# Rows gathered as 128-byte float32 features into four buffers, and turned two slots at a time

## The chip, the cores and the metric

The kernel runs on one core of one Trainium2 chip. The metric is the time of one execution on the device, in microseconds (us). Engines are named PE (TensorE, matrix products), DVE (VectorE), ACT (ScalarE), POOL (GpSimd) and SP (SyncE); ns are nanoseconds.

## The reference

A graph of 3125 nodes with 32 features each and 100000 edges, sorted by their destination `dst`, goes through four layers. Each layer adds its result to `x` and normalizes.

```python
def edge_mlp(x, src, dst):                     # layer 0
    msg = concat([x[dst], x[src] - x[dst]])    # 64 numbers an edge
    h = relu(msg @ W1 + b1); h = relu(h @ W2 + b2); h = relu(h @ W3 + b3)
    return segment_mean(h @ W4 + b4, dst)

def gcn(x, src, dst):                          # layers 1 and 2: weighted sums over edges
    return segment_sum(scaled(x)[src], dst)    # layer 2: then @ weight + bias, relu

def gatv2(x, src, dst):                        # three times in layer 3
    xl, xr = x @ Wl, x @ Wr                    # 8 heads of 32
    logits = (leaky_relu(xl[src] + xr[dst]) * att).sum(-1)
    alpha = softmax over the edges of one dst
    return segment_sum(alpha * xl[src], dst).mean(heads) + bias
```

The three attention layers have a self loop for each node, a residual and a batch norm.

## The kernel before

Nodes lie in 25 windows of 128 (`W`). The edges are cut into blocks of 256 that belong to one window of destinations each; a block has two slots of 128 edges, one edge to a partition. Eight slots are a group, and there are `G` = 104 groups (832 slots). All loops below run over groups.

An edge needs the features of its source. There are two ways to them. **Gather:** POOL issues one indirect DMA for each slot (`DMA_INDIRECT`), which fetches for each of the 128 partitions the row of `table` that its entry of `idx` names. **Dense reading:** PE multiplies a one-hot matrix of the edges' sources (made by DVE from `r_dram`) with the whole table in SBUF, 12 bf16 matmuls, and DVE picks and sums one of seven candidates. `table` in DRAM has rows of `TAB` = 80 float32: 32 features, and behind them the same features as three bf16 parts (hi, mid, lo) whose sum is the float32 number. 

The features of the destination come from windows: SP loads the three parts of a group's four windows (`load_windows`, tile `xwin`), and PE multiplies them with a one-hot matrix of the destinations (`turned`), 12 matmuls for each group.

**Edge pass** (`pool_edges`, `sp_pass0`, `act_pass0`, `pe_pass0`; 104 steps). Seven of a group's slots are gathered (L368) into one of three buffers `rows`, the eighth is read densely (L811, L1478, L1483) into `one0`. `rows_in` of PE turns the group into bank 0 of PSUM: sources of side 0 on partitions 0 to 31 and of side 1 on 64 to 95, destinations on 32 to 63 and 96 to 127. A row slot is turned by three bf16 matmuls with 128x32 weights against `identb`, one for each part (L831); the dense one by a float32 product (L835). The order of these and of the window matmuls (L827) is the list `TURNS`, which alternates rows and windows and the two sides, so that they use different columns of the array. ACT copies the bank to `xT`; three layers of products follow (L842, L847, L855), and a product with the one-hot matrix of the destinations sums the group (L864), which DVE adds to `acc`.

**Convolutions** (twice). 72 groups are gathered whole by POOL (L398) into four buffers, 32 groups are read densely (L900).

**Attention** (three layers, `pool_attention`, `sp_attention`, `act_attention`, `pe_attention`, `attention` of DVE). POOL gathers a group (L381) into one of two buffers: 8 slots of even groups, 7 of odd ones, whose eighth is read densely (`stationary_one`, `read_one` L1029, `pick_one` L1756 and L1759). A buffer is free when PE has turned it (`x_made`, `rows_in` with `TURNS`, L974, L980, L986) and ACT has copied its features to `xs` (`keep`, L651, semaphore `xs_kept`). Step u of PE is, in order: half of the projection (`z_half`, L994), the self loops in the first steps, in even steps the dense reading of group u+3, the first half of the weighted sums of group u-10 (L1055), in odd steps `linear` (L1005), the second `z_half`, `rows_in` of group u+1, the second half of the sums, in odd steps the logits (L1015). Each 8 groups are a chunk; at its end DVE scans the logits for the maxima and PE turns them back and forth (L1099, L1107, L1117). The last 10 steps have sums alone. Between layers the sums become features (`pe_attention_out`), the batch norm runs, and `give_table` of DVE makes the parts for the next layer's table; `store_table` of SP stores it, and POOL waits for that store.

Each engine runs its own program in a fixed order; semaphores tie them. POOL's whole program after the start is gathers and waits. SP's queue has, for attention step u, the four windows and two halves of `turned` of group u+2 and the two halves of `hot` (one-hot matrices) of group u-8.

Of the kernel before, what the change touches and what calls it, by code (L numbers as in the profile page):

```python
# [25 lines left out]
P = 128  # L26
# [34 lines left out]
TAB = C + 3 * C // 2  # L61
# [6 lines left out]
TURNS = [x for i in range(2) for x in [("row", 2 * i, 0), ("window", i, 0), ("row", 2 * i, 1), ("row", 2 * i, 2), ("window", i, 1),  # L68
                                       ("row", 2 * i + 1, 0), ("row", 2 * i + 1, 1), ("window", i, 2), ("row", 2 * i + 1, 2)]]
# [4 lines left out]
def build(nc, x, edge_blocks, L0, W_gcn, b_gcn, gat, out):  # L74
    with ExitStack() as ctx:
# [3 lines left out]
        def sem(name):  # L79
# [29 lines left out]
        rows = sb("rows", [P, 3, 8, TAB])  # L109
        x0_dram = nc.dram_tensor("x0_dram", [P, W * C], F32).ap()  # L110
# [9 lines left out]
        identb = sb("identb", [P, P], BF16)  # L120
# [37 lines left out]
        spanhot = sb("spanhot", [P, HALF, GROUPS], BF16)  # L158
# [57 lines left out]
        one0 = o1[:, 2064:2064 + 4 * C].rearrange("p (b c) -> p b c", b=4)  # L216
# [4 lines left out]
              for k in range(2)]  # L221
        rows4 = [rows[:, 0, :, :], rows[:, 1, :, :]] + [o0[:, 5120 + 640 * k:5120 + 640 * (k + 1)].rearrange(
            "p (j c) -> p j c", j=8) for k in range(2)]
# [10 lines left out]
        tabC = o0[:, 1024:1024 + W * 48].bitcast(BF16).rearrange("p (w c) -> p w c", w=W)  # L234
        cand = o0[:, 2224:2224 + GROUPS * C].rearrange("p (g c) -> p g c", g=GROUPS)
        bt1 = [o0[:, 2560 + 1024 * k:2560 + 1024 * (k + 1)].bitcast(BF16).rearrange("p (k n e) -> p k n e", k=FOLD, n=4)
               for k in range(2)]
        rline1 = [T2[:, :, :].rearrange("p w c -> p (w c)")[:, 64 + 256 * k:320 + 256 * k].bitcast(F16) for k in range(2)]
        hotb = o1[:, 2560:3584].bitcast(BF16).rearrange("p (b j n) -> p b j n", b=2, j=8)
        rowparts = [rows[:, b, :, :].rearrange("p j c -> p (j c)").bitcast(BF16).rearrange("p (j c) -> p j c", j=8)  # L240
                    for b in range(3)]
# [41 lines left out]
        gathered = [sem(f"gathered{b}") for b in range(3)]  # L283
        rows_in3 = [sem(f"rows_in3_{b}") for b in range(3)]
        x0_stored, x0_in = sem("x0_stored"), sem("x0_in")
# [33 lines left out]
        r1_in = [sem(f"r1_in{b}") for b in range(2)]  # L319
        bt1_made, one_read, one_picked, one_kept = sem("bt1_made"), sem("one_read"), sem("one_picked"), sem("one_kept")  # L320
        tab_kept = sem("tab_kept")
# [16 lines left out]
        scaled, norm_turned, x_given, tab_copied = sem("scaled"), sem("norm_turned"), sem("x_given"), sem("tab_copied")  # L338
# [16 lines left out]

        def rows_there(l, g):

            n = l * G + g
            return rows_in3[n % 2], 16 * sum(8 - k % 2 for k in range(n % 2, n + 1, 2))

        def pool_edges(pool):

            pool.wait_ge(table_stored, 16)
            for g in range(G):
                if g >= 3:
                    pool.wait_ge(x0_made, 4 * (g - 2))
                for j in range(7):
                    pool.indirect_dma_start(  # L368
                        rows[:, g % 3, j, :], None, table,
                        bass.IndirectOffsetOnAxis(ap=idx[:, 8 * g + j:8 * g + j + 1], axis=0)).then_inc(gathered[g % 3], 16)  # L370

        def pool_attention(pool, l):

            pool.wait_ge(table_stored, 16 * (l + 4))
            for g in range(G):
                n = l * G + g
                if n >= 2:
                    pool.wait_ge(x_made, 4 * (n - 1))
                    pool.wait_ge(xs_kept, n - 1)
                for j, s in enumerate(piece_slots(g)[0:8 - g % 2]):  # L380
                    pool.indirect_dma_start(  # L381
                        rows[:, n % 2, j, :], None, table,
                        bass.IndirectOffsetOnAxis(ap=idx[:, s:s + 1], axis=0)).then_inc(rows_in3[n % 2], 16)
# [46 lines left out]
        def load_windows(sp, codes, at, b):  # L430

            code = sp.value_load(codes[0:1, at], min_val=0, max_val=(1 << 20) - 1)
            for k in range(4):
                w = window_of(sp, code, k)
                sp.dma_start(xwin[:, b, k, :], table[bass.ds(w * P, P), C:TAB].bitcast(BF16)
                             ).then_inc(xwin_in[b], 16)

        def sp_pass0(sp):
# [23 lines left out]
            def windows_for(g):  # L462
                if g >= G:
                    return
                if g >= 2:
                    sp.wait_ge(x0_made, 4 * (g - 1))
# [25 lines left out]
        def sp_attention(sp, l):  # L492
            sp.wait_ge(table_stored, 16 * (l + 4))

            def rows_for(g):
                b, c, n = g % 2, g // 8, piece_of(g)
                if l * G + g >= 2:
                    sp.wait_ge(x_made, 4 * (l * G + g - 1))
# [15 lines left out]
            def numbers_for(c):  # L514
                if c >= CHUNKS:
                    return
                at = l * CHUNKS + c
                if at >= 2:
                    sp.wait_ge(bt1_made, FOLD * (at - 1))
                first = CHUNK * c + CHUNK // 2 + 4 * PIECE + PIECE - 1  # L520
                sp.dma_start(rline1[at % 2].rearrange("p (n e) -> p n e", n=4),
                             r_dram.rearrange("a (f e) -> (a f) e", f=2)[first:first + 13:4, :].partition_broadcast(P)
# [1522 lines left out]
```

## Time and profile before

| | |
|---|---|
| timed runs, median of 3 | 5986.88 us (5984.18 to 5997.32) |
| profiled execution, span (no other time of it is shown) | 7770.9 us |
| PE busy | 5760.6 us, 43965 matmuls |
| DVE busy | 3565.2 us |
| ACT busy | 1748.7 us |
| POOL busy | 4059.1 us, 4236 instructions |
| edge pass, convolutions, attention begin (first gather) | 52.6, 1331.8, 3218.2 us |

The profiled execution is longer than a timed run, by 30%. Times of single instructions are from it. A time line has start and length in us, the engine, the line of the kernel, output<-input, the count of instructions merged, and in brackets the idle time before them and what ended it; "issue" there means that nothing the profile shows was waited for, "remote" or "another core or an unknown queue" that the releaser isn't among what was recorded. A float32 matmul counts as two instructions, a float32 transpose as one. Ends of matmuls are modelled and overlap the next start; distances between starts are the safer measure.

### The profile page before, as it was taken

To read this page: it belongs to the slowest core of one execution; us is meant where nothing else is said; L and a number is where in the kernel's file an instruction comes from. 1 tells how busy PE (TensorE), PEld (TensorE's weight loads), DVE (VectorE), ACT (ScalarE), POOL (GpSimd) and SP (SyncE) were. 2 spreads that over 40 slices of the span, in tenths; PEclk is the share of its full clock that TensorE was granted. 3 is DMA by queue.
4 is the path that set the end of the run, shared out by engine and by line. 5 is a ranking of instruction groups with operands and counts; after the bars stand their busy time and mean duration, and the time that the engine had idled before them with its cause. 6 is when DMAs were issued, how large, how long until landed. Compare 5 with 4: busy or idle time off the path is not lost.

```text
span 7770.9 us, 130521 instructions
## 1 busy us (share of the span) xinstructions
PE 5760.6 (74%) x43965; PEld 3691.2 (48%) x43965; DVE 3565.2 (46%) x6811; ACT 1748.7 (23%) x3748; POOL 4059.1 (52%) x4236
## 2 busy tenths in 40 slices
PE   5888886566646666578887876877787758788777
PEld 4666665455545454334444443444444424444444
DVE  5444444455544444444444444444444534444446
ACT  2222222344420000022222221222222122222221
POOL 4555554666646566455555533555555245555551
PEclk8888887777767776688888897888888878888988
DMA  4444443222212222233333332333333223333332
GB/s 103 129 129 129 128 128 98 51 56 56 56 47 56 55 56 55 49 82 93 88 91 88 89 85 56 90 90 89 92 89 89 80 58 92 89 89 93 91 88 65
DMA packets 688913, 648.23 MB, mean 83 GB/s; under 512 B 401396, under 2 KB 483771, under 8 KB 688251
## 3 DMA queue, kind: packets, MB, share of 16 engines
q1 hardware_dynamic: 548266, 463.96, 20.0%
q0 software_dynamic: 135616, 175.22, 11.8%
q8 instruction: 357, 5.85, 0.3%
q14 instruction: 306, 2.50, 0.1%
q10 hardware_dynamic: 4368, 0.70, 0.1%
HBM read 550.21 MB, written 89.17 MB: 82 GB/s over the span
## 4 chain that ended last, share of the span: by engine, by line
PE 43%; issue 22%; another core or an unknown queue 21%; DVE 9%; ACT 3%; DVEq 2%; DMA 0%; POOL 0%; ACTq 0%; POOLq 0%
PE ps L1055 14%; PE ps L900 7%; PE ps L994 5%; PE ps L1005 2%; PE ps L1015 2%; PE ps L855 2%; PE ps L915 1%; PE ps L980 1%; DVE region L1778 1%; DVE acc L1803 1%; PE ps L974 1%; PE ps L864 1%; ACT region L662 1%; PE ps L811 1%
## 5 line engine op out<-in xcount | busy, mean ns | idle before, releaser
L381 POOL DMA_INDIRECT rows<-table,idx x2340 | 2258.3, 965 | 2221.5 <-ACT region L651 1042.6
L1055 PE MATMUL ps<-region,hot 128*128 128x272 f32 x4992 | 1528.3, 457 | 295.8 <-DVE region L1756 159.4
L1055 PEld LDWEIGHTS ps<-region,hot 128*128 128x128 f32 x4992 | 1040.8, 219 | 690.9 <-issue 461.8
L1803 DVE TENSOR_TENSOR acc<-acc,ps 128x272 f32 x1248 | 544.5, 436 | 1685.6 <-remote 808.6
L662 ACT ACTIVATE region<-ps 128x512 f32<-128x512 f32 x1248 | 677.3, 595 | 2691.7 <-remote 1438.8
L900 PE MATMUL ps<-hot,region 128*128 128x192 bf16 (+1 forms) x6144 | 896.1, 309 | 444.2 <-issue 429.0
L900 PEld LDWEIGHTS ps<-hot,region 128*128 128x128 bf16 x6144 | 703.4, 123 | 590.9 <-issue 529.9
L368 POOL DMA_INDIRECT rows<-table,idx x728 | 696.6, 957 | 534.2 <-PE ps L835 320.4
L994 PE MATMUL ps<-xT,wcat 64*128 64x512 f32 x2496 | 771.8, 696 | 170.4 <-issue 92.1
L1778 DVE TENSOR_TENSOR region<-ps,region 128x1056 f32<-128x1056 f32 x582 | 724.7, 1251 | 44.0 <-issue 40.4
L398 POOL DMA_INDIRECT rows<-table,idx x576 | 546.6, 949 | 378.5 <-issue 157.3
L398 POOL DMA_INDIRECT region<-table,idx x576 | 548.3, 952 | 342.5 <-issue 158.1
L980 PE MATMUL ps<-identb,rows 128*32 128x128 bf16 x7020 | 405.7, 236 | 290.9 <-issue 251.5
L980 PEld LDWEIGHTS ps<-identb,rows 128*32 128x32 bf16 x7020 | 263.1, 102 | 625.7 <-issue 624.8
L974 PE MATMUL ps<-turned,xwin 128*32 128x256 bf16 x3744 | 394.8, 304 | 133.7 <-issue 131.1
L994 PEld LDWEIGHTS ps<-xT,wcat 64*128 64x128 f32 x2496 | 211.5, 204 | 550.0 <-issue 525.8
L1635 DVE TENSOR_TENSOR region<-ps,gmask 128x448 f32<-128x448 f32 x256 | 158.7, 620 | 620.9 <-remote 551.9
L709 ACT ACTIVATE region<-iota,region 128x128 bf16<-128x128 f32 x832 | 254.1, 389 | 536.4 <-remote 394.5
L1015 PE MATMUL ps<-region,attblk 128*32 128x512 f32 x2496 | 323.7, 627 | 8.0 <-ACT region L662 5.1
L855 PE MATMUL ps<-w,region 128*128 128x64 f32 x1664 | 293.1, 349 | 21.6 <-ACT region L641 15.9
L855 PEld LDWEIGHTS ps<-w,region 128*128 128x128 f32 x1664 | 276.1, 259 | 50.8 <-ACT region L641 43.4
L1615 DVE TENSOR_TENSOR acc<-acc,ps 128x96 f32 (+1 forms) x832 | 192.1, 231 | 228.0 <-issue 77.3
(304 smaller groups left out, 6646.9 us busy)
## 6 DMA issues: line engine op xcount, KB each, us to landing
hot<-hot_dram SPq DMA_DIRECT2D x624, 256.0 KB
turned<-turned_dram SPq DMA_DIRECT2D x624, 128.0 KB
rows<-table,idx POOLq DMA_INDIRECT x3644
hot_dram<-hot SPq DMA_DIRECT2D x104, 512.0 KB
xwin<-table SPq DMA_DIRECT2D x1664, 24.0 KB
region<-hot_dram SPq DMA_DIRECT2D x64, 512.0 KB
region<-d_dram SPq DMA_DIRECT2D x104, 256.0 KB
turned_dram<-turned SPq DMA_DIRECT2D x104, 256.0 KB
```

Source lines behind the costliest of these rows:

```text
L368: pool.indirect_dma_start(rows[:, g % 3, j, :], None, table, bass.IndirectOffsetOnAxis(ap=idx[:, 8 * g + j:8 * g + j + 1], axis=0)).then_i ...
L381: pool.indirect_dma_start(rows[:, n % 2, j, :], None, table, bass.IndirectOffsetOnAxis(ap=idx[:, s:s + 1], axis=0)).then_inc(rows_in3[n % ...
L398: pool.indirect_dma_start(rows4[at % 4][:, j, :], None, table, bass.IndirectOffsetOnAxis(ap=idx[:, 8 * g + j:8 * g + j + 1], axis=0)).then ...
L662: act.activation(rz[g % 2][:, 2 * t + side, :], ps[:, Z + side, :], ACT.Relu).then_inc(rz_made, 1)
L855: mm = pe.matmul(ps[:, 7, j * HID:(j + 1) * HID], h2[:, at:at + P], w3[:, :], start=True, stop=True)
L900: mm = pe.matmul(ps[:, GB + i % 2, 224 * j:224 * j + n], bt[b][:, k, at:at + P], tabparts[:, k::FOLD, (2 + s) * C:(3 + s) * C], start=(k = ...
L980: mm = pe.matmul(ps[q:q + C, XT, j * P:(j + 1) * P], rowparts[(l * G + g) % 2][:, at, 2 * C + s * C:2 * C + (s + 1) * C], identb[:, :], st ...
L994: pe.matmul(ps[:, Z + side, :], wcat[l][q:q + 64, side, t * P:(t + 1) * P], xT[q:q + 64, g % 2, :], start=True, stop=True).then_inc(z_summ ...
L1015: pe.matmul(ps[at:at + 32, LG, :], attblk[l][:, t, (3 - m) * H:(7 - m) * H], rz[g % 2][:, 2 * t + side, :], start=False, stop=(m == 3 and ...
L1055: mm = pe.matmul(ps[:, sum_bank(k, side, i), 0:PC + H], hot[:, b, 4 * side + 2 * i + j, :], px[b][:, 4 * side + 2 * i + j, :], start=(j == ...
L1778: v.tensor_tensor(to, at.unsqueeze(3).broadcast_to([P, 4, H, HK]), xs[:, (k // 8) % 2, k % 8, 4 * side:4 * side + 4, :].unsqueeze(2).broad ...
L1803: v.tensor_tensor(at, at, ps[:, sum_bank(k, side, i), 0:PC + H], ALU.add).then_inc(att_added, 1)
```

## The change

- The edge pass gathers rows of 32 float32 (128 bytes) straight from the input `x`; each attention layer from an array of its own, `feats[l]`, to which SP stores `X`. `table` holds the three bf16 parts alone (`TAB` = 48 float32, 192 bytes), for the windows and the convolutions.
- `rows` has four buffers (`RING`), in the edge pass and in the attention; each slot has 64 columns, of which the upper 32 stay zero after one clearing at the start. `place` puts the slots of side 0 on even and of side 1 on odd places, so that two neighbours together are 128 columns.
- PE turns two slots at once with a float32 transpose of 128x128 (`turn_rows`, four for each group, with zeros where the destinations go), and the window matmuls write their quarters behind it (`turn_windows`).
- The dense reading in the attention is gone, with its one-hot matrices, its DMAs and its picks; POOL gathers 8 slots of each group there. The edge pass keeps its dense reading of the eighth slot, whose sum goes into the row buffer.
- ACT's copy of the features into the table is gone. The copy of X for the end comes from `feats[0]`.

```diff
-TAB = C + 3 * C // 2
+TAB = 3 * C // 2
+RING = 4
+TURN = 3
+WINDOWS = [(side, i, s) for i in range(2) for s in range(3) for side in range(2)]
...
+        feats = [nc.dram_tensor(f"feats{l}", [W * P, C], F32).ap() for l in range(LAYERS)]
...
-        rows = sb("rows", [P, 3, 8, TAB])
+        rows = sb("rows", [P, RING, 8, 2 * C])
...
+        def place(j):
+            return 2 * (j % 4) + j // 4
...
         def pool_edges(pool):
-            pool.wait_ge(table_stored, 16)
+            pool.wait_ge(rows_cleared, 1)
             for g in range(G):
-                if g >= 3:
-                    pool.wait_ge(x0_made, 4 * (g - 2))
+                if g >= RING:
+                    pool.wait_ge(x0_made, TURN * (g - RING + 1))
                 for j in range(7):
                     pool.indirect_dma_start(
-                        rows[:, g % 3, j, :], None, table,
+                        rows[:, g % RING, place(j), 0:C], None, x,
...
         def pool_attention(pool, l):
-            pool.wait_ge(table_stored, 16 * (l + 4))
+            pool.wait_ge(feats_stored, 16 * (l + 1))
             for g in range(G):
                 n = l * G + g
-                if n >= 2:
-                    pool.wait_ge(x_made, 4 * (n - 1))
-                    pool.wait_ge(xs_kept, n - 1)
-                for j, s in enumerate(piece_slots(g)[0:8 - g % 2]):
+                if n >= RING:
+                    pool.wait_ge(x_made, TURN * (n - RING + 1))
+                    pool.wait_ge(xs_kept, n - RING + 1)
+                for j, s in enumerate(piece_slots(g)):
                     pool.indirect_dma_start(
-                        rows[:, n % 2, j, :], None, table,
+                        rows[:, n % RING, place(j), 0:C], None, feats[l],
...
             for l in range(LAYERS):
+                sp.wait_ge(x_given, 3 + l)
+                sp.dma_start(feats[l].rearrange("(w p) c -> p w c", p=P), X[:, :, :]).then_inc(feats_stored, 16)
                 store_table(sp, 3 + l)
...
+        def turn_rows(pe, bank, b, made):
+            for j in range(4):
+                mm = pe.transpose(ps[:, bank, j * P:(j + 1) * P], rows[:, b, 2 * j:2 * j + 2, :].rearrange("p a c -> p (a c)"),
+                                  ident[:, :])
+            mm.then_inc(made, 1)
+
+        def turn_windows(pe, bank, b, made):
+            for side, i, s in WINDOWS:
+                q = 64 * side
+                mm = pe.matmul(ps[q + C:q + 2 * C, bank, 2 * i * P:2 * (i + 1) * P], xwin[:, b, 2 * side + i, s * C:(s + 1) * C],
+                               turned[:, b, (4 * side + 2 * i) * P:(4 * side + 2 * i + 2) * P], start=(s == 0), stop=(s == 2))
+                if i == 1 and s == 2:
+                    mm.then_inc(made, 1)
...
-                for kind, j, s in TURNS:
...
+                turn_rows(pe, XT, g % RING, x_made)
+                turn_windows(pe, XT, b, x_made)
...
-            def read_one(g):
...
-            def stationary_one(l, c, k):
...
-            def pick_one(l, g):
...
-            v.tensor_copy(tabC, tabparts[:, :, 2 * C:5 * C]).then_inc(tab_kept, 1)
```

## Rows read from the trace of the kernel before

**Rows 1.** The page: its first line, and part 4 by engine

```profile
span 7770.9 us, 130521 instructions
PE 43%; issue 22%; another core or an unknown queue 21%; DVE 9%; ACT 3%; DVEq 2%; DMA 0%; POOL 0%; ACTq 0%; POOLq 0%
```

**Rows 2.** Groups by line: count | busy us, mean ns | idle before

```profile
L381 POOL DMA_INDIRECT rows<-table,idx x2340 | 2258.3, 965 | 2221.5 <-ACT region L651 1042.6 <-issue 784.5 <-DMA table<-hot 319.7
L368 POOL DMA_INDIRECT rows<-table,idx x728 | 696.6, 957 | 534.2 <-PE ps L835 320.4 <-issue 192.4 <-DMA table<-hot 19.5
L398 POOL DMA_INDIRECT region<-table,idx x576 | 548.3, 952 | 342.5 <-issue 158.1 <-PE ps L927 129.2 <-remote 55.2
L398 POOL DMA_INDIRECT rows<-table,idx x576 | 546.6, 949 | 378.5 <-issue 157.3 <-PE ps L927 128.4 <-remote 55.4
L980 PE MATMUL ps<-identb,rows 128*32 128x128 bf16 x7020 | 405.7, 236 | 290.9 <-issue 251.5 <-DMA rows<-table,idx 38.5
```

**Rows 3.** Waits of POOL: us in total, times, longest

```profile
POOL rows L381 <- ACT region L651: 1042.6, 254, 10.6
POOL rows L381 <- DMA table<-hot: 319.7, 3, 131.8
POOL rows L368 <- issue: 192.4, 626, 0.6
```

**Rows 4.** Gathers of two lines: duration ns min/median/max

```profile
L381 POOL DMA_INDIRECT rows<-table,idx x2340: 938/944/1928, 3218.2 to 7639.8; - x195
...
L415 POOL DMA_INDIRECT region<-in_edge_blocks,block_no x4: 937/942/1134, 28.2 to 32.2; - x4
```

**Rows 5.** Time line of POOL: start us, us, instruction, [idle before <- releaser]

```profile
52.63 0.94 POOL L368 DMA_INDIRECT rows<-table,idx  x1 [19.53 <-DMA table<-hot]
...
106.63 0.94 POOL L368 DMA_INDIRECT rows<-table,idx  x1 [27.47 <-PE ps L835]
...
1262.91 0.94 POOL L368 DMA_INDIRECT rows<-table,idx  x1 [0.30 <-issue]
...
1331.75 0.95 POOL L398 DMA_INDIRECT rows<-table,idx  x1 [28.73 <-DMA table<-hot]
...
2217.36 0.94 POOL L398 DMA_INDIRECT region<-table,idx  x1 [0.30 <-issue]
...
2268.94 0.95 POOL L398 DMA_INDIRECT rows<-table,idx  x1 [8.67 <-DMA table<-hot]
...
3218.17 0.94 POOL L381 DMA_INDIRECT rows<-table,idx  x1 [57.22 <-DMA table<-hot]
...
4738.70 0.94 POOL L381 DMA_INDIRECT rows<-table,idx  x1 [130.66 <-DMA table<-hot]
...
7639.78 0.95 POOL L381 DMA_INDIRECT rows<-table,idx  x1 [0.30 <-issue]
```

**Rows 6.** Time line of PE, and of DVE for the last row

```profile
3856.34 1.21 PE L1029 MATMUL ps<-region 128*128 128x224 bf16 x12
...
4120.30 0.60 PE L1107 MATMUL ps<-ident,region 128*128 128x128 f32 x4
...
4120.83 0.64 PE L1015 MATMUL ps<-region,attblk 128*32 128x512 f32 x4
...
4613.92 1.13 PE L994 MATMUL ps<-xT,wcat 64*128 64x512 f32 x4
...
4618.07 0.23 PE L980 MATMUL ps<-identb,rows 128*32 128x128 bf16 x2
...
4618.90 2.10 PE L1055 MATMUL ps<-region,hot 128*128 128x272 f32 x8
...
4620.93 1.13 PE L994 MATMUL ps<-xT,wcat 64*128 64x512 f32 x4
...
4629.95 0.50 PE L1055 MATMUL ps<-region,hot 128*128 128x272 f32 x1
...
4728.57 0.98 DVE L1267 CAST hot<-X 128x800 bf16<-128x800 f32 x1
```

More of the change, by code:

```diff
@@ L221, in build @@
               for k in range(2)]
-        rows4 = [rows[:, 0, :, :], rows[:, 1, :, :]] + [o0[:, 5120 + 640 * k:5120 + 640 * (k + 1)].rearrange(
-            "p (j c) -> p j c", j=8) for k in range(2)]
+        rows4 = [o0[:, 5120 + 8 * TAB * k:5120 + 8 * TAB * (k + 1)].rearrange("p (j c) -> p j c", j=8) for k in range(4)]
         parts4 = [r.rearrange("p j c -> p (j c)").bitcast(BF16).rearrange("p (j c) -> p j c", j=8) for r in rows4]
@@ L282, in build @@
         idx_made = sem("idx_made")
-        gathered = [sem(f"gathered{b}") for b in range(3)]
-        rows_in3 = [sem(f"rows_in3_{b}") for b in range(3)]
-        x0_stored, x0_in = sem("x0_stored"), sem("x0_in")
+        rows_at = [sem(f"rows_at{b}") for b in range(RING)]
+        rows_cleared = sem("rows_cleared")
+        feats_stored, x0_in = sem("feats_stored"), sem("x0_in")
         hot_made = sem("hot_made")
@@ L434, in load_windows @@
                 w = window_of(sp, code, k)
[L435 removed]
+                sp.dma_start(xwin[:, b, k, :], table[bass.ds(w * P, P), :].bitcast(BF16)
                              ).then_inc(xwin_in[b], 16)
@@ L820, in rows_in @@
                 pe.wait_ge(xwin_in[b], 64 * (g // 2 + 1))
[L821 removed]
+                pe.wait_ge(*edge_rows(g))
                 pe.wait_ge(one0_kept, g + 1)
[L823 to L838 removed]
+                turn_rows(pe, 0, g % RING, x0_made)
+                turn_windows(pe, 0, b, x0_made)
             def first_layer(g):
@@ L1051, in sums_half @@
                         pe.wait_ge(att_added, of_bank)
-                    if side == 1 and i == 0:
-                        pe.wait_ge(one_picked, (l * G + min(k + LAG + 4, G)) // 2)
                     for j in range(2):
@@ L1296, in give_table @@
             def give_table(of, first=False):
-                hi, mid, lo = (tabparts[:, :, (2 + k) * C:(3 + k) * C] for k in range(3))
-                if first:
-                    cp(tab[:, :, 0:C], of)
-                else:
+                hi, mid, lo = (tabparts[:, :, k * C:(k + 1) * C] for k in range(3))
+                if not first:
                     v.sem_inc(x_given, 1)
@@ L1319, in _ @@
             v.memset(X[:, W - 1, :], 0.0).then_inc(x_zeroed, 1)
+            v.memset(rows[:, :, :, :], 0.0).then_inc(rows_cleared, 1)
             v.memset(zeros[:, :], 0.0).then_inc(zeros_made, 1)
@@ L1480, in pick0 @@
                 v.wait_ge(one0_picked, g + 1)
-                if g >= 4:
-                    v.wait_ge(x0_made, 4 * (g - 3))
-                v.tensor_reduce(one0[:, g % 4, :], cand0.rearrange("p g c -> p c g"), AX.X, ALU.add).then_inc(one0_kept, 1)
+                if g >= RING:
+                    v.wait_ge(x0_made, TURN * (g - RING + 1))
+                v.tensor_reduce(rows[:, g % RING, place(7), 0:C], cand0.rearrange("p g c -> p c g"), AX.X, ALU.add).then_inc(one0_kept, 1)
             def bias0(g):
@@ L1863, in attention @@
                         link(v.tensor_tensor(at, at, fscale[:, :].unsqueeze(2).broadcast_to([P, H, HK]), ALU.mult))
-                    def pick():
-                        if u % 2 == 0 and u + 3 < G:
-                            pick_one(l, u + 3)
-                    if phase in (3, 4) and u // 8 + 1 < CHUNKS:
-                        for q in range(2):
-                            stationary_one(l, u // 8 + 1, 2 * (phase - 3) + q)
                     if phase == 0 and ends:
@@ L1916, in _ @@
                 give_table(X[:, :, :])
[L1917 to L1925 removed]
+                for i in range(QUADS):
                     n = min(4, W - 4 * i)
```

175 lines of the change are left out of this document (19 added, 156 removed).

## The prediction

> **What bounds the kernel now.** I read the page's parts 1 and 4 first, then the groups, the waits of POOL, and time lines of POOL and PE.
>
> Its execution took 7770.9 us over its span, and the page shows nothing around that; the timed runs have a median of 5986.88 us, 0.770 of it. So 1784 us exist only under the profiler. The chain names PE first, but gives 21% (about 1630 us) to "another core or an unknown queue", and this program has one core [rows 1]. I read that share as PE held up while it is recorded, and take no duration from a stretch in which PE stutters. What I need is an engine whose times don't depend on PE's stutter. That is POOL.
>
> POOL issues 4220 gathers: 728 in the edge pass, 1152 in the two convolutions, 2340 in the attention [rows 2]. One takes 0.957, 0.949 to 0.952 and 0.965 us on average [rows 2], and the next begins 0.307 us later when nothing is to be waited for (192.4/626) [rows 3]. Gathers only: 728 x 1.264 + 1152 x 1.257 + 2340 x 1.272 = 920 + 1448 + 2976 = 5344 us. POOL is without gathers up to 52.6 us, then 67.9 (1263.9 to 1331.8), 50.6 (2218.3 to 2268.9), 319.7 in sum before the first gathers of the three layers [rows 3], and 130.2 us at the end, together 621; and 27.5 us in which three filled buffers wait for PE's first step [rows 5]. 5344 + 621 + 28 = 5993 us, against 5987 timed. All other waits of POOL in this trace (1043 us of them for the ACT copy that frees a buffer [rows 3]) have no room in a timed run. That it fits to 6 us is partly luck; that it fits to 1% says that POOL sets the time of the kernel without a profiler, if its spacing is the same there.
>
> PE is close behind. The cleanest stretch is the end of a layer, where its records come without a gap: an even step takes 4613.92 to 4620.93 = 7.01 us, an odd one to 4629.95 = 9.02 us, the latter without the row turns (0.83 us, 4618.07 to 4618.90) and without the dense reading (12 matmuls, 1.21 us to the end of the last; I take 1.1) [rows 6]. In sum 18.0 us for two steps, 9.0 a step; four groups of four turns for each chunk of 8 steps, at 0.53 us [rows 6], add 0.3 a step. POOL needs 7.5 x 1.272 = 9.5 us a step. The two are within 3%, POOL ahead.
>
> **The change, part by part.**
>
> *Dense reading out of the attention.* Each odd group gathers 8 rows instead of 7: 52 more in each layer, 156 in all, 156 x 1.272 = +198 us on POOL. In exchange PE loses 1872 matmuls (1.1 us x 156 = 172 us, 0.55 a step) and DVE three instructions for each reading. PE and DVE stand beside POOL, so this is worth nothing while POOL bounds.
>
> *128-byte rows in place of 320-byte ones.* One would hope for cheaper gathers. The trace has one of another size: the four gathers of edge blocks fetch 4096 bytes for each partition and take 0.942 us in the median, where those of table rows take 0.944 [rows 4]. The issue doesn't depend on the bytes. I take 0, bounds -0.01 and +0.01 us a gather. The traffic saved (192 bytes a row) lies on DMA engines that are no one's bound.
>
> *Whole-array turns.* PE loses 21 to 24 bf16 turns of a step (7020 in the attention [rows 2], 104 x 21 in the edge pass) and a float32 one; four float32 transposes of two slots each come in. Four such transposes take 0.53 us from the first to the next group (4120.30 to 4120.83) [rows 6]. The twelve window matmuls stay, but no longer beside row turns: at the reading's pace of about 0.09 us for 208 columns, 256 columns take 0.11 us, in six pairs 0.65 us. So 1.2 us where 0.83 stood, +0.35 us a step: fewer instructions, no less array time. Bounds: -1.2 us, if PE outside the profiler is held by the count of instructions, not by columns, and +0.8 us, should the windows run singly. I take +0.35. A step of attention then needs 9.3 - 0.55 + 0.35 = 9.1 us of PE against 8 x 1.272 = 10.2 of POOL.
>
> Of this the Trainium skill, TensorEngine Tiling, section Key Properties, says that changing the tiling mode, and not only the tile, drains the engine. The new order has one change of mode more in a step of attention (64x128, 128x128, 128x32). The trace agrees as far as it goes: after the last of four transposes the next mode begins 0.2 us later, where they follow each other at 0.11. That drain is inside the 0.53 us; by the page alone the direction would be the same, a costlier row turn.
>
> *Four buffers in place of three (edge) and two (attention).* Where POOL bounds it never waits for a buffer, and more of them don't speed it. They do help once: before the first edge step POOL stood 27.5 us with its buffers full [rows 5]; now it issues 7 more gathers in that time, 7 x 1.264 = -9 us. Between layers nothing can be fetched ahead, as the rows don't exist.
>
> *A table of rows of its own for each layer.* POOL waits for its store, issued when X is complete, instead of for the parts table. The first cast begins at 4728.57, the table's store waits for it and three more operations (four of 1 us each), and the gathers began at 4738.70 [rows 6, 5]; the new store can go some 4.2 us earlier, so -4.2 x 3 = -13 us. SP has one store more ahead of the table's, 0.4 us to issue; PE's first step needs both and still has 10 us of gathers to wait for. The gathers of the edge pass no longer wait for a table either, about 3 us earlier, but then into the same wait for PE.
>
> *The smaller edits.* ACT's copy of X into the table (0.9 us, beside DVE's casts), DVE's copy of the parts, a cast, the clearing of the row buffers at the start (beside the load of the edges): 0, bounds -5 and +5. The convolution's table is 0.6 MB instead of 1 MB: -3 us for two stores, bounds -8 and 0.
>
> Sum: 5987 + 198 - 9 - 13 - 3 = 6160 us. One term pulls it down. Gathers in the attention average 0.965 us over a median of 0.944; if all of this excess goes with the DVE work removed, 2496 x 0.021 = -52. I take a third: **6140 us**, +2.6%. In the profiled execution the sum runs otherwise. There PE is what is held up, and about 9900 of its matmuls go (7020 + 104 x 21 turns, 1872 in the readings, 520 for the eighth slots; 1664 transposes come); a step of 13.3 us (7639.8 - 3218.2, less the two pauses between layers, 319.7 - 57.2, over 312 [rows 5, 3]) falls to POOL's 10.2 and a little, so that its span should be 6500 to 7100 us, much shorter than 7771. Profile shorter, kernel slower.
>
> The Trainium skill, GPSIMD Engine Reference, section Key points, says that POOL shares its SBUF interfaces with VectorE and contends with instructions of the 2-port mode or with two SBUF inputs. No row here ties a long gather to a DVE instruction; by the page the excess should shrink, the sum would be 6108.
>
> **Rivals.**
>
> *A. PE bounds, and POOL's spacing is partly the profiler's.* If the 0.305 us between gathers is mostly recording, POOL needs 7.7 us a step after, and PE decides. For it: the chain, and 1043 us in which POOL waited for buffers that PE and ACT hold. Against it: PE's clean steps make 9.3 x 312 = 2900 us; with 649 around the gathers 2438 us are left for the edge pass and the convolutions, and their gathers alone need 2368 at the trace's spacing, but only 1790 without the 0.307. So three stages would have to miss POOL's time from above by chance. Time: by columns 312 x (0.35 - 0.55) + 104 x 0.35 - 13 - 9 = -48, 5940 us; if the count of instructions decides, up to -1.2 us a step of 416, 5987 - 500 - 172 = 5315, which the 4376 gathers, at 0.95 us and 600 us around them (4760), allow. The likelier end is the first; a middle spacing near 1.15 us also ends there.
>
> *B. POOL bounds, but at 1.20 us or so without the profiler.* Then 9.6 us a step after, against 9.5 before (PE and POOL together): +30 to +60 less 25, 5990 to 6020: hardly to be told from no change.
>
> *C. The turn costs more than it seems.* The side of slower, but by PE: the windows run after the transposes with a drain on each side, +0.8 us on 416 steps = +333, less 172 and 22: 6125 us. It decides once a PE step passes POOL's 10.2, so 1.1 us above my 9.1. The trace's drains of 0.2 us speak against that.
>
> *D. The change doesn't do what it says:* four buffers are of no use if the order of the queue still ties POOL to the step before. This is so under the forecast anyway, and costs the 9 us.
>
> **How the numbers follow.** Forecast 0.54; A 0.32; B 0.10; C 0.04. Of this kernel, about 0.2% (12 us) can be told from no change. Slower: 0.54 + 0.04 + half of B = 0.63; same 0.05; faster 0.32. The forecast's own range is 6085 to 6175: the terms' bounds, and a spacing at the median of 1.249 instead of the mean (4376 x 0.018 = -79) at its foot. To hold 8 in 10 the range reaches into the first half of A: 5890 to 6180.
>
> **What would show it.** Right: in the profile after, gathers still 0.94 us with 0.30 between, in the attention back to back with no wait for an ACT copy; 10.1 us a step; PE with gaps that end on gathers; the first gather of a layer about 6 us after X. The four transposes about 0.5 us and the windows 0.65. Wrong: a gather issue that is visibly shorter for 128 bytes; POOL waiting for buffers in spite of four; or a timed run below 5975, which can't be with 4376 gathers at 1.25 us and 600 us outside them (6070): then the spacing under the profiler isn't the kernel's.

## The result and the profile after

The changed kernel takes **6056.62 us** (median of 4 runs, 6054.66 to 6073.31) against 5992.10 for the kernel before on the same chip (4 runs): a ratio of 1.0117, interval 1.0100 to 1.0134. It is slower, as forecast, but by 64.5 us and not by 153: inside the range that was to hold 8 in 10 (5890 to 6180), below the forecast's own (6085 to 6175).

The page of the kernel after: its first line, part 4 by engine, and three groups.

```profile
span 6055.0 us, 109647 instructions
POOL 48%; issue 25%; PE 17%; DVE 7%; DVEq 2%; ACT 1%; ACTq 1%; DMA 0%; POOLq 0%
L375 POOL DMA_INDIRECT rows<-feats,idx x2496 | 2394.4, 959 | 1023.4 <-issue 759.4
L771 PE MATMUL ps<-ident,rows 128*128 128x128 f32 x1664 | 270.7, 287 | 320.4 <-DMA rows<-feats,idx 295.2
L779 PE MATMUL ps<-turned,xwin 128*32 128x256 bf16 x4992 | 363.0, 283 | 0.0
```

Its waits of POOL, and one of PE (us in total, times, longest):

```profile
POOL rows L375 <- issue: 759.4, 2491, 0.3
POOL rows L375 <- DMA feats<-X: 263.4, 3, 117.2
POOL rows L375 <- ACT region L627: 0.6, 2, 0.3
PE ps L771 <- DMA rows<-feats,idx: 295.2, 230, 16.6
```

Its time line of POOL (start us, us, instruction, the idle time before it and its releaser):

```profile
99.97 0.94 POOL L362 DMA_INDIRECT rows<-in_x,idx  x1 [13.36 <-PE ps L779]
...
3710.03 0.94 POOL L375 DMA_INDIRECT rows<-feats,idx  x1 [117.19 <-DMA feats<-X]
...
4877.64 0.94 POOL L375 DMA_INDIRECT rows<-feats,idx  x1 [117.05 <-DMA feats<-X]
...
5929.39 0.94 POOL L375 DMA_INDIRECT rows<-feats,idx  x1 [0.30 <-issue]
```

The time line of PE in a step of its attention:

```profile
3025.75 1.13 PE L945 MATMUL ps<-xT,wcat 64*128 64x512 f32 x4
3027.58 0.63 PE L771 MATMUL ps<-ident,rows 128*128 128x128 f32 x4 [0.70 <-DMA rows<-feats,idx]
3028.14 0.83 PE L779 MATMUL ps<-turned,xwin 128*32 128x256 bf16 x12
3028.90 2.10 PE L989 MATMUL ps<-region,hot 128*128 128x272 f32 x8
```

How they are read beside the rows of before. The profiled execution of after isn't stretched: its span and the timed runs agree. The stutter behind the 7770.9 us of [rows 1] isn't in it, and with it went "another core or an unknown queue". The attention's gathers still take 0.94 us (mean 0.959, 0.965 before [rows 2]) and follow each other after 0.30 us: 2491 of 2496 waited for nothing else, where 254 waited for a buffer in the stretched execution of before [rows 3]. So GpSimd does set the attention's pace after, and TensorE waits 295 us for rows. The turn with its windows takes 3028.90 - 3027.58 = 1.32 us, where 0.83 stood [rows 6].

A comparison by stages needs an undistorted profile of before. The first experiment, `before_ring4`, gives one: it is timed like before, and its span is 5983.2. From its profile and that of after, by the first gather of each stage (us):

```
stage                             before, 4 buffers  after     difference
start to first convolution        1051.4             1039.8    -11.6
both convolutions                 1510.7             1502.0     -8.7
layer 1 (with the pause behind)   1136.5             1168.2    +31.7
layer 2                           1143.1             1167.6    +24.5
layer 3 to the end                1141.5             1177.4    +35.9
sum                               5983.2             6055.0    +71.8
```

All the loss lies in the attention, 92 us in 312 steps. The first difference is the least certain one: in the six undistorted profiles of variants of before, whose edge pass is the same, the first convolution begins at 1045.9 to 1066.3 us.

### The profile page after: what moved, and what is told of

Its sections match the earlier page's. It is cut to its first block, busy times and chain, and to the rows that moved or that the text cites. A ratio compares the mean times of both kernels' runs of the same rounds, so it can differ in the third digit from the quotient of the medians.

```text
span 6055.0 us, 109647 instructions
## 1 busy us (share of the span) xinstructions
PE 4879.0 (81%) x34033; PEld 3210.5 (53%) x34033; DVE 3385.8 (56%) x6326; ACT 1790.5 (30%) x3743; POOL 4198.1 (69%) x4392
## 4 chain that ended last, share of the span: by engine, by line
POOL 48%; issue 25%; PE 17%; DVE 7%; DVEq 2%; ACT 1%; ACTq 1%; DMA 0%; POOLq 0%
POOL rows L375 39%; PE ps L869 10%; POOL rows L362 9%; DVE region L1575 2%; PE ps L896 1%; DVE region L1553 1%; PE ps L884 1%; DVEq L1527 1%; DVE acc L1533 1%; PE ps L833 1%; PE ps L824 1%; ACTq L714 1%; DVEq L1533 1%; PE ps L989 0%; PE ps L794 0%
## 5 line engine op out<-in xcount | busy, mean ns | idle before, releaser
L375 POOL DMA_INDIRECT rows<-feats,idx x2496 | 2394.4, 959 | 1023.4 <-issue 759.4
L989 PE MATMUL ps<-region,hot 128*128 128x272 f32 x4992 | 1304.9, 405 | 86.5 <-DVE acc L1696 75.1
L392 POOL DMA_INDIRECT region<-table,idx x1152 | 1092.4, 948 | 384.2 <-issue 350.5
L989 PEld LDWEIGHTS ps<-region,hot 128*128 128x128 f32 x4992 | 903.3, 190 | 499.4 <-issue 302.4
L362 POOL DMA_INDIRECT rows<-in_x,idx x728 | 701.3, 963 | 251.4 <-issue 220.4
L869 PE MATMUL ps<-hot,region 128*128 128x192 bf16 (+1 forms) x6144 | 742.5, 292 | 24.1 <-issue 22.9
L771 PE MATMUL ps<-ident,rows 128*128 128x128 f32 x1664 | 270.7, 287 | 320.4 <-DMA rows<-feats,idx 295.2
L896 PE MATMUL ps<-region 128*128 128x96 bf16 x1152 | 94.8, 242 | 524.4 <-issue 360.3
L771 PEld LDWEIGHTS ps<-ident,rows 128*128 128x128 f32 x1664 | 184.4, 147 | 570.9 <-issue 570.7
L779 PEld LDWEIGHTS ps<-turned,xwin 128*32 128x32 bf16 x4992 | 220.2, 99 | 93.5 <-issue 73.3
```

The lines of the kernel that those rows point to most:

```text
L362: pool.indirect_dma_start(rows[:, g % RING, place(j), 0:C], None, x, bass.IndirectOffsetOnAxis(ap=idx[:, 8 * g + j:8 * g + j + 1], axis=0) ...
L375: pool.indirect_dma_start(rows[:, n % RING, place(j), 0:C], None, feats[l], bass.IndirectOffsetOnAxis(ap=idx[:, s:s + 1], axis=0)).then_in ...
L392: pool.indirect_dma_start(rows4[at % 4][:, j, :], None, table, bass.IndirectOffsetOnAxis(ap=idx[:, 8 * g + j:8 * g + j + 1], axis=0)).then ...
L771: mm = pe.transpose(ps[:, bank, j * P:(j + 1) * P], rows[:, b, 2 * j:2 * j + 2, :].rearrange("p a c -> p (a c)"), ident[:, :])
L779: mm = pe.matmul(ps[q + C:q + 2 * C, bank, 2 * i * P:2 * (i + 1) * P], xwin[:, b, 2 * side + i, s * C:(s + 1) * C], turned[:, b, (4 * side ...
L869: mm = pe.matmul(ps[:, GB + i % 2, 224 * j:224 * j + n], bt[b][:, k, at:at + P], tabparts[:, k::FOLD, s * C:(s + 1) * C], start=(k == 0 an ...
```

## The experiments

Each is timed beside the kernel before. The median of before was 5986.6 us beside experiments 1 to 4, 5989.7 beside 5 to 8 and 5993.0 beside 9 to 11, so that a difference between two experiments is good to a few us. The edits are shown in part; where a kernel has other buffers than the one it starts from, the text says so.

**1. before_ring4:** the attention of before with the four buffers alone.

```
-        rows = sb("rows", [P, 3, 8, TAB])
+        rows = sb("rows", [P, 4, 8, TAB])
...
-                if n >= 2:
-                    pool.wait_ge(x_made, 4 * (n - 1))
...
+                if n >= 4:
+                    pool.wait_ge(x_made, 4 * (n - 3))
...
```

> The kernel before with four row buffers instead of two in the attention; all else as before. Theory 1 (POOL's gathers plus its pauses make the time; the gain that offset half of the 156 extra gathers came from waits for buffers that the kernel before still had): about 80 us less than before, 5915 us, between 5890 and 5935. Rival 2 (POOL never waited for buffers in a timed run, as the prediction had it; the offset came from shorter heads and tails): within 10 us of before, 5985 to 6000.

Measured: 5984.97 us, 1.0001 (0.9988 to 1.0013). Theory 1 falls: no time was lost to buffers. Rival 2's number came; its shorter heads and tails are the 20 us ahead of the attention in the table above. The chain of the page, now undistorted, names TensorE, where that of after names GpSimd:

```profile
PE 50%; issue 19%; POOL 18%; DVE 9%; DVEq 2%; ACT 1%; DMA 1%; ACTq 1%; POOLq 0%
```

Its waits of GpSimd in the attention:

```profile
POOL rows L381 <- issue: 698.9, 2268, 3.0
POOL rows L381 <- DMA table<-hot: 328.6, 3, 147.7
POOL rows L381 <- ACT region L651: 21.8, 64, 1.4
```

GpSimd hardly waits within a layer, yet between layers it stands 147.7 us; after the change it is 117.2. Of these 30 us 6 are the earlier store. From the first cast that follows a finished X to the first gather, before_ring4 takes 10.1 us and after 4.0, in each of the three layers:

```profile
3688.50 0.98 DVE L1267 CAST hot<-X 128x800 bf16<-128x800 f32 x1
3698.63 0.94 POOL L381 DMA_INDIRECT rows<-table,idx  x1 [145.93 <-DMA table<-hot]
```

and in after, whose first gather (3710.03) stands above:

```profile
3706.01 0.98 DVE L1191 CAST hot<-X 128x800 bf16<-128x800 f32 x1
```

The other 24 fit a GpSimd that with four buffers is some groups ahead at a layer's end, so that TensorE works off what was gathered. TensorE was late, not GpSimd.

**2. after_no_eighth:** after, eighth row of odd groups neither gathered nor read.

```
-                for j, s in enumerate(piece_slots(g)):
+                for j, s in enumerate(piece_slots(g)[0:8 - g % 2]):
```

> The kernel after, but the eighth row of the odd groups in the attention is neither gathered nor read densely (the buffer keeps what is in it, so that part of the result is left out): 156 gathers fewer. Theory 1: 156 x 1.264 = 197 us less than after, 5860 us (5850 to 5875), since PE at about 9.1 us a step still lies under POOL's 7.5 x 1.264 = 9.5. Rival 2 (PE takes over as soon as POOL is relieved): 5900 to 6000.

Measured: 5869.67 us, 0.9801 (0.9783 to 0.9820): 187 below after, 156 gathers at 1.20. After is held by gathers. And it is 117 us below before, with the same number of gathers. Some 17 us of that lie ahead of the attention; the rest says that before was held by something else.

**3. after_ring2:** after with two buffers in the attention.

```
-                if n >= RING:
-                    pool.wait_ge(x_made, TURN * (n - RING + 1))
...
+                if n >= 2:
+                    pool.wait_ge(x_made, TURN * (n - 1))
...
```

> The kernel after with two row buffers instead of four in the attention. Theory 1 in the form of the prediction (a POOL that bounds doesn't wait for buffers): within 15 us of after, 6050 to 6070. Rival (a POOL that bounds on average still loses time at the ends of chunks, where PE holds both buffers): 60 to 100 us more than after, 6115 to 6155.

Measured: 6099.16 us, 1.0186 (1.0167 to 1.0205). The third and fourth buffer are worth 42.5 us here and nothing in before: they let GpSimd go on where TensorE is held for a moment, which pays only for the engine that sets the pace on average. Neither theory's range held it (Theory 1 came within 30 us, the rival within 16).

**4. after_dense:** after, with the dense reading back (rows turned the new way).

```
+                if u >= 8 and u % 2 == 0 and u + 3 < G:
+                    if k > 0:
+                        pe.wait_ge(att_added, 4 * (l * G + k) - 1)
+                    read_one(u + 3)
```

> The kernel after with the dense reading of the eighth row of odd groups put back in the attention (its sum goes into the row buffer, as in the edge pass): 156 gathers fewer, 1872 matmuls and 468 picks and one-hots more. Theory 1: POOL still bounds on average at 9.5 us a step beside PE at 9.1 + 0.55 = 9.65, so the two share it and some of the 197 us is lost: 5880 us, 5860 to 5930. Rival 2 (the dense reading costs PE as much as the gathers cost POOL): 5985 to 6060.

Measured: 6064.28 us, 1.0129 (1.0109 to 1.0148). Its gathers are those of before, its turn the new one, and it is 78 us above before. From the first gather of the attention to the end it takes 3521.2 us, before_ring4 3421.1. If TensorE bounds in both, the new turn costs it 100 us there, 0.32 us a step on average over all steps. Theory 1 (5880) is out by far, and rival 2's range (to 6060) is missed by 4 us.

**The new theory.** From the records of each kernel I took the time from ACT's copy of one group's turned rows to the next (mean over three layers, groups 16 to 95, by g%8, us). PE turns group g in its step g-1, so column g goes from the second half of step g-1 into step g:

```
                    0      1      2      3      4      5      6      7     mean
before_ring4       9.80  10.30  11.86  11.15   9.75   8.03   9.75   8.03   9.83
after             10.32  10.46  10.96   9.75   9.90   9.71  10.07   9.87  10.13
after_no_eighth    9.41  10.27  11.07   9.53   9.38   8.55   9.38   8.55   9.52
after_dense       10.35  10.34  11.94  11.61  10.35   8.52  10.35   8.52  10.25
```

Eight steps are a chunk, and the columns 0 to 3 hold its boundary: scans on VectorE, transposes and sums on TensorE. In before a step takes TensorE 9.83 us, above the 9.53 of 7.5 gathers (0.965 + 0.305 us each); after, 8 gathers at 1.264 make 10.11 and the measured step is 10.13. In these groups TensorE stands idle for rows 0.03 us a chunk in before_ring4 and 5.2 us in after. Theory 3: TensorE bounds before, GpSimd after.

**5. before_short_read:** before (two buffers), one of the reading's 12 matmuls left.

```
-                for k in range(FOLD):
+                for k in range(1):
...
-                    for s in range(3):
+                    for s in range(1):
...
```

> The kernel before, with the dense reading of the attention cut to 1 of its 12 matmuls (the eighth rows of the odd groups are then incomplete: part of the result is left out); gathers, turns, waits and buffers are untouched. Theory 3 (before: TensorE holds the attention at about 9.80 us a step, GpSimd's 7.5 gathers at 9.53 stand just behind; after: GpSimd holds it at 10.11 and TensorE is at about 9.6): TensorE falls by about 0.5 us a step, GpSimd takes over at 9.53, so 104 x 3 x 0.27 = 84 us less, 5900 us (5885 to 5925). Rival 1 (the prediction's: GpSimd's gathers set the time before): no change, 5980 to 5990. A third possibility, TensorE alone with nothing close behind: 104 x 3 x 0.5 = 156 less, 5830.

Measured: 5903.96 us, 0.9871 (0.9849 to 0.9892), as Theory 3 has it; the step is 9.56 us, against 9.53 for the gathers.

**6. before_7rows:** before (two buffers), with 155 gathers fewer.

```
-                for j, s in enumerate(piece_slots(g)[0:8 - g % 2]):
+                for j, s in enumerate(piece_slots(g)[0:8 if n == 0 else 7]):
```

> The kernel before, in whose attention the even groups gather 7 rows instead of 8 too (155 gathers fewer, 7 a step; the eighth row of even groups is a stale one: part of the result is left out); TensorE's work is untouched. Theory 3 (TensorE holds the attention before): no change, 5975 to 5990; at most some us where a chunk starts. Rival 1 (GpSimd's gathers hold it, 1.27 us each): 155 x 1.27 = 197 us less, about 5790.

Measured: 5969.26 us, 0.9969 (0.9958 to 0.9981): 20 us less where the prediction's own bound asks for 197, and 6 us below Theory 3's range. Most of the saving lies at the head of each layer: its first 16 steps take 144 to 148 us instead of 150 to 151, and all later steps 9.82 to 9.83 as in before_ring4. GpSimd now waits for buffers 264 us:

```profile
POOL rows L381 <- ACT region L651: 264.1, 172, 3.9
```

**7. after_turn2:** after, its four transposes made twice.

```
+                for j in range(4):
+                    pe.transpose(ps[:, XT, j * P:(j + 1) * P], rows[:, g % RING, 2 * j:2 * j + 2, :].rearrange("p a c -> p (a c)"),
+                                 ident[:, :])
                 turn_rows(pe, XT, g % RING, x_made)
```

> The kernel after, in whose attention the four whole-array transposes of each group are done twice (the same values into the same places): 4 x 0.107 = 0.43 us more of TensorE a step. Theory 3 (GpSimd holds the attention after at 10.11 us a step, TensorE needs about 9.6): 10.0 is still under 10.11, so 0 to +15 us, 6057 to 6072. Rival (TensorE's turns hold the attention after as well, the gathers only beside it): 312 x 0.43 = +134 us, 6190.

Measured: 6058.14 us, 1.0122 (1.0103 to 1.0141): 1.5 us more than after, where the rival asks for 134. TensorE has 0.4 us of room in a step of after.

**8. before_3of8:** before with four buffers, one reading in four replaced by a gather.

```
+        def reads(g):
+            return g % 8 in (1, 3, 5)
```

> The kernel before with four row buffers in the attention, and the dense reading in 3 of 8 groups instead of 4 of 8: the fourth gathers its eighth row (39 gathers more, 39 readings fewer; result complete). Theory 3: TensorE 9.80 - 0.14 = 9.66 us a step, GpSimd 7.625 x 1.264 = 9.64: balanced, 312 x 0.14 = 44 us less, 5943 us (5935 to 5965), faster than both kernels. Rival 1 (GpSimd's gathers hold the time before): 39 x 1.27 = 50 us more, 6037.

Measured: 5992.46 us, 1.0015 (1.0001 to 1.0029). Missed by 49 us. Column 4, which lost its reading, fell from 9.75 to 8.78 us; column 3 rose from 11.15 to 11.95 and took most of it back. The time line of TensorE in a column 3 of before_ring4:

```profile
3230.31 3.56 PE L1055 MATMUL ps<-region,hot 128*128 128x272 f32 x8 [2.55 <-DVE region L1756]
...
3234.86 2.10 PE L1055 MATMUL ps<-region,hot 128*128 128x272 f32 x8
```

VectorE ahead of those sums:

```profile
3225.91 0.23 DVE L1261 TENSOR_SCALAR fscale<-ps,first_hot 128x8 f32<-128x8 f32 x1 [4.22 <-PE ps L1088]
...
3227.46 1.26 DVE L1778 TENSOR_TENSOR region<-ps,region 128x1056 f32<-128x1056 f32 x1
...
3229.78 0.38 DVE L1756 TENSOR_TENSOR region<-ps,spanhot 128x224 f32<-128x224 f32 x1
```

The busy times and the granted clock (PEclk) of that stretch of TensorE:

```profile
core 0: us, PE busy (x) PEld busy (x) DVE busy (x) ACT busy (x) POOL busy (x), PEclk, DMA share, GB/s
3230.00:3234.00 4.00, 3.69 (x10) 2.66 (x12) 2.30 (x4) 0.00 (x0) 3.08 (x4) 0.58 0.18 31
```

The same place of a chunk in before_3of8, its time line and the busy times with the clock (columns as above):

```profile
3384.16 3.38 PE L1061 MATMUL ps<-region,hot 128*128 128x272 f32 x8 [2.55 <-DVE region L1762]
```

and

```profile
3384.00:3387.50 3.50, 3.34 (x10) 2.13 (x10) 2.15 (x4) 0.00 (x0) 2.59 (x4) 0.61 0.20 35
```

The eight sums wait 2.55 us for VectorE, and they then take 3.4 to 3.6 us instead of 2.1: the granted clock is 0.58 and 0.61 there, a mix of the two levels, 1.2 and 2.4 GHz, after 2.55 us without work. What they wait for is the pick of the reading (L1756): the sums' second half waits for it by semaphore (`one_picked`), as readings and sums write one bank of PSUM. In phase 2 of a chunk VectorE comes to the pick late. It waits for TensorE's L1088, scales the sums at the boundary, makes the products and two additions, and the pick stands behind them. The readings 1, 3 and 5 keep just this pick (it belongs to g%8=5).

Sums begun at half clock (0.45 us apart instead of 0.23; counted above 0.40) number 115 in before_ring4 and 207 in before_3of8. The clock records of the 30 columns 3 in groups 16 to 95 say more. The wait is 2.54 to 2.97 us in all of them; a fall to the lower level comes with it in 9 of 30 in before_ring4 and in 24 of 30 in before_3of8, and such a column takes 12.3 us on average, one without a fall 10.6 to 10.7. The 15 more falls are the whole rise from 11.15 to 11.95. Why they come more often there is open.

**9. before_moved:** before with four buffers and the same four readings; the one of phase 2 and its pick come a step later, and the sums of phase 2 no longer wait for it. Its expectation and the next two call this reading of the wait Theory 4.

```
-                        pe.wait_ge(one_picked, (l * G + min(k + LAG + 4, G)) // 2)
+                        pe.wait_ge(one_picked, (l * G + min(k + LAG + 4 - 2 * (k % 8 == 0), G)) // 2)
...
-                if u >= 8 and u % 2 == 0 and u + 3 < G:
+                if u >= 8 and (u % 2 == 0 and phase != 2 and u + 3 < G or phase == 3 and u + 2 < G):
...
-                        if u % 2 == 0 and u + 3 < G:
+                        if u % 2 == 0 and phase != 2 and u + 3 < G:
                             pick_one(l, u + 3)
+                        elif phase == 3 and u + 2 < G:
+                            pick_one(l, u + 2)
```

> The kernel before with four row buffers in the attention, in which the dense reading and the pick that fall in phase 2 of every chunk (for the group g%8=5) are made one step later, in phase 3; the amount of work is the same and the result complete. Theory 4 (TensorE holds the attention before at 9.83 us a step because VectorE's work at the chunk boundary, with the pick in it, makes TensorE wait some 2.6 us in phase 3, after which its clock drops): steps of phase 2 and 3 go from 11.9 and 11.1 us to about 10.9 and 10.0, the chunk from 78.6 to about 76.6, 9.57 a step, just over GpSimd's 9.51: 104 x 3 x 0.26 = 80 us less, 5905 us (5895 to 5930). Rival (TensorE's sum of work sets the step, wherever its readings lie): no change, 5980 to 5990.

Measured: **5930.61 us**, 0.9896 (0.9875 to 0.9916): 62 below before, the fastest complete version and 126 below after. Its forecast range ended at 5930. Columns 2 and 3 go from 11.86 and 11.15 to 10.90 and 10.47, the mean to 9.62; forecast were 10.9, 10.0 and 9.57. Half-clock sums fall from 115 to 40, and no column 3 of groups 16 to 95 has a fall of the clock (9 of 30 before). These falls cost 1.7 us each, so 39 chunks get back about 20 us from the clock; this is an estimate from the two kinds of column. The rest is the wait ahead of the sums, which shrank. PE's waits in before_ring4:

```profile
PE ps L1055 <- DVE region L1756: 85.1, 33, 3.0
```

and in before_moved, whose time line shows one of them:

```profile
PE ps L1055 <- DVE region L1778: 47.3, 33, 1.8
```

```profile
3229.25 2.07 PE L1055 MATMUL ps<-region,hot 128*128 128x272 f32 x8 [1.41 <-DVE region L1778]
```

After a wait of 1.41 us the sums take their full-clock 2.07 us. The wait that is left is for the products (L1778), not for the pick.

**10. before_3of8b:** as 8 (four buffers), but the reading left out is the one of phase 2.

```
-            return g % 8 in (1, 3, 5)
+            return g % 8 in (1, 3, 7)
```

> As the kernel with 3 of 8 readings, but the reading left out is the one in phase 2 of a chunk (g%8=5) and not the one in phase 4 (g%8=7); g%8=5 gathers its eighth row instead; result complete. Theory 4: TensorE's step falls to about 9.45, GpSimd's 7.625 x 1.266 = 9.65 takes over: 104 x 3 x 0.18 = 56 us less, 5930 us (5920 to 5945). Rival (as above): like the first one with 3 of 8, 5977 to 5992.

Measured: 5970.46 us, 0.9951 (0.9933 to 0.9968), 22 us better than 8, 40 short of the forecast. It missed both the forecast's range and the rival's. The step did fall to 9.71 (forecast 9.65; 7.625 gathers at this run's 1.272 us are 9.70), and no column 3 has a fall of the clock. But in the profiled execution the pause of GpSimd from the edge pass to the convolution was 72.1 us, against 54.4 in before_ring4: 18 of the 40 us lie there. The edge pass, whose code is the same, ended at a lower clock. The 40 us from 990 in before_3of8b and then in before_ring4 (columns as above):

```profile
990.00:1030.00 40.00, 35.93 (x196) 28.54 (x194) 8.77 (x23) 5.92 (x7) 3.25 (x4) 0.50 0.16 51
```

and

```profile
990.00:1030.00 40.00, 29.77 (x296) 25.39 (x294) 17.45 (x48) 9.14 (x13) 7.58 (x7) 0.81 0.21 63
```

That pause varies in the other variants of before too (53.1 to 64.9 us); what sets the clock at the end of the edge pass is open.

**11. after_2of8:** after, with the readings of g%8=1 and 7 put back.

```
+        def reads(g):
+            return g % 8 in (1, 7)
```

> The kernel after, with the dense reading of the eighth row in 2 of 8 groups (g%8=1 and 7, neither of them read in phase 2); result complete. GpSimd falls to 7.75 x 1.264 = 9.80 us a step, TensorE rises from 9.52 to 9.52 + 2 x 0.97 / 8 = 9.76. Theory 4: 104 x 3 x (10.12 - 9.80) = 100 us less than the kernel after, 5955 us (5945 to 5975), and so some 30 less than before. Rival (a reading costs its full part wherever it lies and TensorE is held by the sum of its work, 10.25 with 4 of 8): (10.25 + 9.52)/2 = 9.89, 5985.

Measured: 5966.15 us, 0.9959 (0.9942 to 0.9975): 90 below after and inside the forecast's range; a step takes 9.85, where the forecast had 9.80 for GpSimd and 9.76 for TensorE, almost alike. Both kernels, before and after, leave one of the two engines room. The split between reading and gathering is a dial, and where the readings lie in the chunk is a second one.

## Why the prediction was wrong

The direction was right for reasons half right; the step that failed is the first, "POOL sets the time of the kernel without a profiler", and within it the term for TensorE's chunk boundary: 0.3 us a step, measured 0.94.

- **What bounded before.** In the attention it was TensorE. The prediction put it at 9.0 + 0.3 = 9.3 us a step, from the end of a layer. The 8.9 us of two steps without a boundary (9.75 and 8.03) confirm its 9.0. The boundary was the error: it was priced by 16 transposes at 0.3 us a step, and costs (43.1 - 4 x 8.89)/8 = 0.94. From the records of before_ring4, TensorE stands idle 4.92 us a chunk (gaps above 0.05 us), in columns 1 to 3 and nowhere else, 0.62 a step; 2.58 of them are the wait for the pick. The falls of the clock add 0.06 (9 in 30 chunks, 1.7 us each), and what is left, 0.27, is what was booked for the transposes. So the term was right for the work and had nothing for the waits, in steps that the rows of the end of a layer don't have. 9.83 lies above 9.53, not under it.
- **The fit of 5993 to 5987** was luck. Its pauses were read from the stretched execution. Up to the attention it counts 2624 us where before_ring4 takes 2562, nearly all of it pauses of GpSimd that are shorter there (54.4 us for 67.9, for one). In the attention it counts 3369 where before_ring4 takes 3421. The two errors, +62 and -52, cancel; and GpSimd's gathers alone, at 9.53 us a step, are within 3% of what TensorE took.
- **The +198 us for 156 gathers.** As a price on GpSimd it holds: 187 us in experiment 2. But the path held TensorE's 9.83 before, so the rise of the time is (10.11 - 9.83) x 312 = 87 us. Measured in the attention are 92: 71 in the groups 16 to 95, 27 in the first 16 steps of the layers, -6 in the rest. This is the miss: 198 was booked against a bound that stood 0.30 us a step (94 us) below the real one. Taking the reading from TensorE was not "worth nothing" either: with it and the new turn TensorE needs 10.25 a step (experiment 4), above GpSimd's 10.11.
- **Gather issue independent of bytes:** right, 0.944 us in the median for 128 bytes and 0.944 to 0.945 for 320. Of the excess of the mean a third was expected to go, 17 us. The mean went from 0.965 to 0.959. But over all profiles it lies at 0.960 to 0.969 with readings in the attention (nine kernels) and at 0.959 to 0.961 without (four): a few ns may come from the work taken off VectorE, and the 6 are within what kernels with the same work differ by. The Trainium skill, GPSIMD Engine Reference, section Key points, tells of a contention between GpSimd and VectorE at their SBUF interfaces. With three VectorE instructions gone for each of 156 readings most of the excess stayed, so that its full 52 us would have been wrong, and no run here shows what the rest is.
- **Spacing under the profiler:** 0.30 us also where the span equals the timed run. That part of rival A falls; that TensorE bounded before, its other half, was true, and that it would after, false (experiment 7).
- **The turn:** 1.32 us against 0.83, so +0.49 where +0.35 was taken; hidden under GpSimd in after, visible in experiment 4 (10.25 against 9.83 a step).
- **Head and tables:** -9, -13 and -3 were forecast. The pause of GpSimd before the first edge step fell from 21.1 us to 13.4 (17.1 to 21.1 in the variants of before), as forecast. At the heads of the layers the gathers begin 6.1 us earlier each, 18 in all where 13 were booked, and the first turned rows are copied 14 us behind the first gather in both kernels, so that the layers do start earlier by as much. The first of these three is in the 8.7 us of the convolutions and leaves 2.6 for the smaller tables.
- **Four buffers:** "Where POOL bounds it never waits for a buffer" was wrong by 42.5 us (experiment 3). An engine that bounds on average still waits where its consumer is slow for a moment.
- **The profiled execution:** 6500 to 7100 us were forecast, 6055.0 came.

## What to carry to other kernels

When two engines stand within 3% of each other, add up a full period of each, with its boundary steps, and not the cleanest stretch; what an edit costs on one engine counts only from where the other one stood. A sum that meets the time to 0.1% doesn't name the bound: a second engine in step with it fits as well. And place movable work so that no other engine waits for it in a step that is already late: at equal work, one reading moved by one step was worth 62 us (its two further buffers were worth nothing in experiment 1).

## What the runs showed of the hardware

- The one profiled execution of the kernel before spans 7770.9 us against 5987 timed, that of the same kernel with four buffers instead of two and as many matmuls 5983.2. No run shows what stretched the first. A stretched execution says little of a timed one; a small variant may give a clean one.
- Waits of TensorE and its granted clock, from columns 3 of groups 16 to 95, 30 for each kernel: waits of 2.54 to 2.97 us were followed by the lower level in 9 (before_ring4) and 24 (before_3of8), waits of 2.02 to 2.39 us in 18 (after_dense), waits of 1.41 to 1.77 us in none (before_moved, before_3of8b). In the fall shown above the clock was 0.58 and the eight matmuls took 1.5 us longer. Waits of 2.55 us passed without a fall as well (one in before_3of8 at 3228.6: 2.07 us for the eight), so the wait alone doesn't decide it.
- An indirect gather of 128 rows is issued each 1.249 us (median of the distances; 1.252 in before_moved and before_3of8b), for rows of 128 and of 320 bytes alike.
